# Two transformer layers on one core: an earlier first restack, idle products in batch 0, products and maxima placed elsewhere

## What is computed

```
# layer A: attention, 16 heads; queries are the normalised x itself (head size 8)
Q = heads(xn);  K = heads(xn @ Wk + bk);  V = heads(xn @ Wv + bv)      # value size 32
o = softmax(Q K^T + causal) V
x = x + (xn + gelu(o) @ Wf + bf)
# layer F: attention, 8 heads of 64, with 8 experts for the values and for the outputs
q, k = xn @ w_q, xn @ w_k;  gates = sigmoid(xn @ w_gate);  sel = argmax(gates)
gm = one_hot(sel) * gates
values = gm-weighted value_experts of xn
out = softmax(q k^T / 8 + causal) values
x = x + sum over heads and experts of gm * (out @ output_experts)
```

## Time and profile before

| | us |
|---|---|
| median of three plain runs (1241.27 to 1246.39) | 1242.96 |
| the profiled execution | 1249.98 |
| its span, first to last instruction | 1248.2 |
| TensorE, matmuls, busy | 1125.7 (90%) |
| TensorE, weight loads, busy | 636.2 (51%) |
| ScalarE busy | 945.1 (76%) |
| VectorE busy | 864.1 (69%) |
| GpSimd busy | 363.9 (29%) |
| mean share of full TensorE clock granted | 0.957 |

### The profile page before, as it was taken

The page is one execution under the profiler, slowest core; times in us unless marked ns, Lnnn a source line. Parts: engine busy times, 40 slices in busy tenths (PEclk is TensorE's granted clock), DMA queues, the critical chain, the costliest instruction groups (busy, mean ns, idle before and its releaser), DMA issues.

```text
span 1248.2 us, 19900 instructions
## 1 busy us (share of the span) xinstructions
PE 1125.7 (90%) x5720; PEld 636.2 (51%) x5720; DVE 864.1 (69%) x2715; ACT 945.1 (76%) x2639; POOL 363.9 (29%) x460
## 2 busy tenths in 40 slices
PE   2697998999989999999989999899999999899998
PEld 1124754357543764347543575437643475435753
DVE  4732878658676687758786686767877597866844
ACT  3874788956989489867889669894898678896651
POOL 1012323242133322342232421343223332323210
PEclk8556999989999999999999999999999999999999
DMA  6201223002320222202230023202222032300220
GB/s 192 67 10 71 69 84 90 11 15 69 111 59 12 58 65 78 59 4 69 86 95 10 20 65 111 59 12 60 64 77 59 4 75 85 91 3 24 56 69 9
DMA packets 43646, 72.73 MB, mean 58 GB/s; under 512 B 9664, under 2 KB 25408, under 8 KB 43216
## 3 DMA queue, kind: packets, MB, share of 16 engines
q1 hardware_dynamic: 42256, 67.26, 20.1%
q10 hardware_dynamic: 1280, 4.20, 1.2%
HBM read 45.34 MB, written 8.80 MB: 43 GB/s over the span
## 4 chain that ended last, share of the span: by engine, by line
PE 42%; ACT 30%; DVE 14%; issue 8%; DMA 3%; SPq 2%; POOL 2%; ACTq 0%; DVEq 0%
ACT masked L899 14%; PE ps_m L679 10%; ACT pt L950 10%; PE ps_o L667 8%; DVE masked L1275 6%; PE ps_max L576 3%; PE ps_exp L576 3%; PE ps_max L788 2%; PE ps_exp L578 2%; PE ps_m L485 2%; ACT s2k L839 2%; DVE val L1468 2%; POOL pt L1142 2%; ACT s2q L839 1%; DVE pt L1449 1%
## 5 line engine op out<-in xcount | busy, mean ns | idle before, releaser
L899 ACT ACTIVATE masked<-masked,low 128x512 f32<-128x512 f32 (+3 forms) x768 | 422.8, 553 | 73.3 <-DVE low L1275 71.6
L1275 DVE CUSTOM_DVE_ANT_0 masked<-ps_max,mask 128x512 f32<-128x512 f32 (+3 forms) x768 | 350.1, 487 | 158.0 <-PE ps_max L576 90.7
L1142 POOL TENSOR_SCALAR_AFFINE_SELECT pt<-pt 128x512 f32<-128x512 f32 (+2 forms) x192 | 144.8, 754 | 560.9 <-ACT pt L950 560.9
L950 ACT ACTIVATE pt<-ps_exp 128x384 f32<-128x384 f32 (+1 forms) x480 | 238.3, 517 | 63.4 <-PE ps_exp L576 35.4
L667 PE MATMUL ps_o<-pt,val 128*32 128x128 f32 (+6 forms) x1536 | 188.0, 471 | 15.4 <-POOL pt L1142 15.4
L576 PE MATMUL ps_max<-s2k,s1q 72*128 72x512 bf16 (+3 forms) x512 | 129.7, 321 | 49.6 <-DVE low L1275 29.3
L679 PE MATMUL ps_m<-at,oe_sb 128*128 128x512 f32 x300 | 157.6, 612 | 1.9 <-DVE at L1326 1.9
L899 ACT ACTIVATION_READ_ACCUMULATOR masked<-masked,low 128x1 f32 x768 | 146.1, 190 | 0.0
L576 PEld LDWEIGHTS ps_max<-s2k,s1q 72*128 72x128 bf16 x512 | 47.0, 99 | 144.7 <-DVE low L1275 72.1
L1326 DVE TENSOR_TENSOR at<-osb,hots 128x512 f32<-128x512 f32 x150 | 104.3, 700 | 14.0 <-PE ps_m L679 14.0
L576 PE MATMUL ps_exp<-s1q,s2k 75*128 75x384 bf16 (+3 forms) x384 | 99.2, 323 | 11.4 <-ACT pt L950 8.6
(11 more groups left out here) (183 smaller groups left out, 1960.8 us busy)
## 6 DMA issues: line engine op xcount, KB each, us to landing
hots<-hot_d SPq DMA_DIRECT2D x48, 256.0 KB, 4.5
s1q<-parts_q SPq DMA_DIRECT2D x96, 96.0 KB
s2k<-parts_k SPq DMA_DIRECT2D x96, 96.0 KB
s1q<-pt SPq DMA_DIRECT2D x64, 128.0 KB, 2.3
s1k<-pt SPq DMA_DIRECT2D x64, 128.0 KB, 2.3
hots<-hot_d ACTq DMA_DIRECT2D x16, 256.0 KB, 4.5
parts_q<-pt SPq DMA_DIRECT2D x24, 128.0 KB, 2.3
parts_k<-pt SPq DMA_DIRECT2D x24, 128.0 KB, 3.8
```

What stands on the lines that cost most here:

```text
L899: last = nc.scalar.activation(e, e, ACT.Exp, bias=low[:, g % 2, c:c + 1], scale=-1.0, accum_out=den[:, g % 2, c:c + 1])
L950: nc.scalar.activation(pt[:, (n % 2) * 4 + j, 0:c1 - c0], score_bank(k, u)[:, c0:c1], ACT.Exp).then_inc(exp_done[k].sem, 1)
L1142: nc.gpsimd.affine_select(out=v, in_=v, compare_op=ALU.is_ge, fill=0.0, base=0, pattern=[[0, HG[k]], [0, m], [1, P]], channel_multiplier=- ...
L1275: last = v.tensor_tensor_reduce(out=masked[:, u % JUNK, c0:c0 + w], in0=src[:, c0:c0 + w], in1=mask[:, S - w:S], scale=-1.0, scalar=POS, o ...
```

## The change

It has six parts. (1) Start: SyncE issues the zeros after the restacking and layer A of batch 0 no longer waits for them; the keys of group 0 of batch 0 are restacked by ScalarE's queue (`first_keys`). (2) Batch 0: Tensor gets `idle_product`, a matmul of constants into ps_m1 whose result nobody reads: six of 512 columns before layer A, one of 256 columns after each of the 36 units at the start, and wherever a later batch has a product of the batch before. (3) The products of layer A sit at other steps, evenly one a stage from step 7 on; the one between the two pieces of the projection goes before it. (4) `FIRST` holds 22 units, two at every step; the units 22 and 23 go on Tensor between the first value tile and the last weighing of layer F, and on Vector and Scalar to the start of layer A (`pre_units`). (5) The value tiles of layer A are spaced out among the units (`VALUE_AT`). (6) The first transposition of layer F uses bank 6.

```diff
 BANK.update({(k, "T", g): 0 for k in "AF" for g in range(GROUPS)})
+BANK["F", "T", 0] = 6
 BANK.update({("A", "V", t): (6, 2, 0, 3)[t] for t in range(T)})
...
 A_UNITS = STAGES * HG["A"]
-FIRST = {FIRST_AT + n: range(24 * n // 11, 24 * (n + 1) // 11) for n in range(11)}
+FIRST_UNITS = 22
+FIRST = {FIRST_AT + n: range(2 * n, 2 * n + 2) for n in range(11)}
...
-def pre_groups(a):
-    return (0, 1, 2) if a == 0 else (2,)
+FIRST_IDLE, IDLE = 6, 256
+VALUE_AT = {2: 0, 3: 1, 5: 2, 7: 3}
+def pre_units(a):
+    first = 0 if a == 0 else FIRST_UNITS
+    return [divmod(u, A_UNITS) for u in range(first, 3 * A_UNITS)]
...
 STEPS_AT = [("F", 14 + 5 * m // 4) for m in range(OUTPUTS_F)] + [("pre", n) for n in (2, 5, 8, 11)]
-STEPS_AT += [("A", u) for u in (1, 2, 4, 6, 8, 10, 13, 15, 18, 21)]
+STEPS_AT += [("A", u) for u in (1, 2, 4, 7, 11, 15, 19, 23, 27, 31)]
 for u, step in enumerate(STEPS_AT):
...
-PRODUCT_AT = 24
-LAST_AT = {36 + n: T * E - TURN + n for n in range(TURN)}
+PRODUCTS_AT = {35: T * E - TURN - 1, 39: T * E - TURN}
+LAST_AT = {(36 + n if n else 33): T * E - TURN + n for n in range(TURN)}
 NEXT_AT, NEXT_X_AT = 44, 28
-SUMS_AT = 6
+SUMS_AT = 8
 HOTS_AT = {4: (0,)}
...
             sp.dma_start(wf_sb[:], wf.rearrange("p (g d) -> p g d", d=D)).then_inc(w_in[1].sem, 16)
-            sp.wait_ge(cst.sem, cst.count(0, 16 * 3))
-            sp.dma_start(s2q[0:64].bitcast(F32).rearrange("p h n -> p (h n)"), zeros_d[0].partition_broadcast(64)
-                         ).then_inc(zero_rows.sem, 16)
...
             parts_to_dram(0, "q")
-            sp.wait_ge(zero_rows.sem, zero_rows.count(0, 16))
             parts_to_dram(0, "k")
+            sp.wait_ge(cst.sem, cst.count(0, 16 * 3))
             sp.wait_ge(parts_out["q"].sem, parts_out["q"].count(0, 16 * PARTS))
...
                 restack_q(g)
-                restack_k(g)
+                if g > 0:
+                    restack_k(g)
+            sp.dma_start(s2q[0:64].bitcast(F32).rearrange("p h n -> p (h n)"), zeros_d[0].partition_broadcast(64)
+                         ).then_inc(zero_rows.sem, 16)
             for b in range(B):
                 layer_a(b)
+                if b == 0:
+                    sp.wait_ge(zero_rows.sem, zero_rows.count(0, 16))
                 one_rows(b)
...
+            def idle_product(columns):
+                mm(ps_m[BANK["F", "acc", 0]][:, 0:columns], ident_sb[:],
+                   wf_sb[:].rearrange("p g d -> p (g d)")[:, 0:columns], start=True, stop=True)
...
+                if f < 0:
+                    idle_product(S)
+                    return
                 if u == 0:
...
                 n_units = STAGES * HG["A"]
-                for g in pre_groups(a):
-                    pe.wait_ge(restacked_a[g].sem, restacked_a[g].count(a, 16 * RESTACK["A"]))
-                    for n in range(n_units):
-                        if a > 0 and 1 <= n < T:
-                            value_a(a, n)
-                        if g == 2 and n == SCORES_AT:
-                            rows_arrived(a, 0)
-                            score_unit("A", a, 0, 0, 0)
-                            score_unit("A", a, 0, 0, 1)
-                        max_unit("A", a, g, n)
-                        if a > 0:
-                            outputs(a - 1, "pre", n)
-                        if a == 0 and g == 1 and n == n_units // 2 - 1:
-                            maxima_transposed("A", a, 0)
+                for n, (g, m) in enumerate(pre_units(a)):
+                    if a > 0 and n < 2:
+                        continue
+                    if m == 0:
+                        pe.wait_ge(restacked_a[g].sem, restacked_a[g].count(a, 16 * RESTACK["A"]))
+                    if a > 0 and VALUE_AT.get(n):
+                        value_a(a, VALUE_AT[n])
+                    if g == 2 and m == SCORES_AT:
+                        rows_arrived(a, 0)
+                        score_unit("A", a, 0, 0, 0)
+                        score_unit("A", a, 0, 0, 1)
+                    max_unit("A", a, g, m)
+                    if a > 0 and g == 2:
+                        outputs(a - 1, "pre", m)
+                    elif a == 0:
+                        idle_product(IDLE)
+                    if a == 0 and g == 1 and m == n_units // 2 - 1:
+                        maxima_transposed("A", a, 0)
                 for g in range(GROUPS):
...
                                 max_unit("A", a, 3, LATE[u])
-                            if a > 0 and OUTPUTS.get(("A", u)):
+                            if OUTPUTS.get(("A", u)):
                                 outputs(a - 1, "A", u)
-                            elif a > 0 and u == PRODUCT_AT:
-                                product(a - 1, T * E - TURN - 1)
+                            elif u in PRODUCTS_AT:
+                                product(a - 1, PRODUCTS_AT[u])
                             if s == 1 and j == 0 and g + 1 < GROUPS:
...
                             weigh("A", a, n - 1)
-                if a > 0:
-                    product(a - 1, T * E - TURN)
+                product(a - 1, T * E - TURN + 1)
                 weigh("A", a, NST - 1)
...
                     value_a(f + 1, 0)
+                    for g, m in pre_units(f + 1)[:2]:
+                        if m == 0:
+                            pe.wait_ge(restacked_a[g].sem, restacked_a[g].count(f + 1, 16 * RESTACK["A"]))
+                        max_unit("A", f + 1, g, m)
                 weigh("F", f, NST - 1)
...
                 f, first = a - 1, T * E - TURN
-                if f >= 0:
-                    product(f, first + 1)
-                project_back(a, (0, 1, 2))
-                if f >= 0:
-                    product(f, first + 2)
-                project_back(a, (3,))
-                if f >= 0:
-                    for u in range(first + 3, T * E - 2):
-                        product(f, u)
+                product(f, first + 2)
+                project_back(a, (0, 1, 2, 3))
+                for u in range(first + 3, T * E - 2):
+                    product(f, u)
                 transposed("F", a)
-                if f >= 0:
-                    product(f, T * E - 2)
-                    product(f, T * E - 1)
+                product(f, T * E - 2)
+                product(f, T * E - 1)
...
                 value_a(0, t)
-            pe.wait_ge(zero_rows.sem, zero_rows.count(0, 16))
             pe.wait_ge(set_v.sem, set_v.count(0, 3))
             pe.wait_ge(set_p.sem, set_p.count(0, 2))
+            pe.wait_ge(w_in[1].sem, w_in[1].count(0, 16 * 3))
+            for n in range(FIRST_IDLE):
+                idle_product(S)
             for b in range(B):
                 attention_a(b)
-                if b == 0:
-                    pe.wait_ge(w_in[1].sem, w_in[1].count(0, 16 * 3))
                 turn(b)
...
                 n_units = STAGES * HG[k]
-                for g in pre_groups(b) if k == "A" else ():
-                    for n in range(n_units):
-                        if g == 2 and n == SCORES_AT:
-                            weights(k, b, 0, 0)
-                            weights(k, b, 0, 1)
-                        denominators(k, b, g, n)
-                        if g == 1 and n == n_units // 2 - 1:
-                            maxima(k, b, 0)
-                    logs(k, b, g)
+                for g, m in pre_units(b) if k == "A" else ():
+                    if g == 2 and m == SCORES_AT:
+                        weights(k, b, 0, 0)
+                        weights(k, b, 0, 1)
+                    denominators(k, b, g, m)
+                    if b == 0 and g == 1 and m == n_units // 2 - 1:
+                        maxima(k, b, 0)
+                    if m == n_units - 1:
+                        logs(k, b, g)
                 if k == "F":
...
+            def first_keys():
+                act.wait_ge(cst.sem, cst.count(0, 16 * 3))
+                act.wait_ge(parts_out["k"].sem, parts_out["k"].count(0, 16 * PARTS))
+                n_rows, h = PARTS * DH, slice(0, HG["A"])
+                for m in range(PARTS):
+                    nc.scalar.dma_start(ks[m * n_rows:(m + 1) * n_rows, h],
+                                        parts_d["k"].rearrange("m d h n -> (m d) h n")[:, h]
+                                        ).then_inc(restacked_a[0].sem, 16)
+                nc.scalar.dma_start(ks[STACK:STACK + PARTS, h], onesb_d.rearrange("p (h n) -> p h n", n=S)[:, h]
+                                    ).then_inc(restacked_a[0].sem, 16)
...
             expert_weights_high()
+            first_keys()
             act.wait_ge(split_lo.sem, split_lo.count(0, 2))
...
                 turn(b)
+                if b == 0:
+                    act.wait_ge(zero_rows.sem, zero_rows.count(0, 16))
                 experts(b)
...
             def attention_a(a):
-                n_units = STAGES * HG["A"]
-                for g in pre_groups(a):
-                    for n in range(n_units):
-                        if a > 0 and n < T:
```

(18 more changed lines are left out.)

## The result

The changed kernel took 1226.22 us as a median of four plain runs (1224.75 to 1228.14), the kernel before 1243.82 beside it; the ratio is 0.9845 [0.9816, 0.9875]. The profiled execution took 1228.14, with a span of 1226.4 against 1248.2. The sign was right, the gain half of what was forecast: 17.6 instead of 36 in the medians, 21.8 instead of 35.8 between the profiled executions.

A forecast was written before the change was run, and what follows sets the result against it. Bounds: the start, batch 0 at 1.2 GHz, short waits of the fullest engine in steady batches. Terms 16.3+3.1+8.8+7.7+4.0 = 39.9, 35.8 after discount: 1214.2 profiled, 1207 plain; range 1191 to 1227.

The forecast's parts named there:

- Start: Opening of batch 0: without the wait for zeros and with a second issuer, Tensor starts earlier; 8.0 taken, 4.4 to 10.7.
- Rival C: Start of batch 0: it doesn't move, as competing restacked rows land in 13 instead of 5.15; 1215, chance 0.07.
- Clock of batch 0: Idle matmuls lift Tensor to 2.4 GHz: 8.9 gained in layer A, 2.4 behind it, 3.0 lost ahead of it.
- Rival B: Batch 0: idle work doesn't lift the clock and is paid at 1.2 GHz on a full engine; 1274, chance 0.04.
- Dip of batch 1: Low-clock dip ahead of batch 1's projection goes with more products in the last steps: 3.1, bounds 0 and 3.1.
- Bank: First transposition of layer F: Tensor's 1.47 wait for Scalar goes, Vector limits the gain; 0.5 a batch, 4.0 in all.
- Two units out: Three-unit steps 18 and 23 of layer F lose their waits: about 1.1 a batch, 7.7 over seven boundaries.
- Products spread: Layer A: fewer products ahead of step 24 shorten Scalar's waits, later ones fit Tensor's waits; 1.1 a batch, 8.8.
- The discount: Last three terms (20.5), gains of neighbouring waits, counted at four fifths, 16.4, as the next fullest engine takes over.
- Rival A: Steady batches stay bound by the fullest engine, only batch 0 gains: 1224, or 1231 with delayed last weights; chance 0.22.
- the two waits of 1.47 and 1.13: Signs in layer F: no 1.47 behind its first transposition, no 1.13 in the eighteenth step.
- the distance of the projections: Sign between two batches' projections: down from 145.4 to about 143; staying at 145 would mark the forecast wrong.

The follow-up runs named there:

- experiment 1: Changed kernel with the products back at their old places, all of part 3 undone, in batch 0 too: 1210.35 us, ratio 0.9709.
- experiment 5: Kernel before the change with only the products moved to the change's new places: 1259.87 us, ratio 1.0122.
- experiment 6: Changed kernel with the first transposition of layer F back in bank 0: 1232.68 us, ratio 0.9891.
- experiment 7: Changed kernel with all 24 units in layer F's steps again, none ahead of the last weighing, value tiles spaced from group 2: 1236.57 us, ratio 0.9918.
- experiment 10: Changed kernel with products at steps 5, 9, ... 37, without the six idle products before layer A and the 36 behind the units: 1204.99 us, ratio 0.9698.

## Why the prediction was half right

*Start: -8.0 forecast, -7.0 measured.* The steps held: key parts issued without waiting for the zeros, landing 3.11 (3.8 taken), restacking from 18.57 (19.7). Only the last landing was not the 5.15 taken over from before, but 7.37. Rival C's mechanism, a longer landing, is there in a small size: 2.2, not 8. In the other nine traces with this start the first maximum is at 25.9 to 27.8, so the forecast of 26.7 lies within what the start does from one execution to the next.

*Clock of batch 0.* The -8.9 for layer A proper is right where the products don't disturb it: with the old places (experiment 1) it is 36.3 in batch 0, 9.3 less than before. Turn and front of layer F gave 3.2 (2.4 forecast), the stretch ahead of the weights cost 2.0 (3.0). In sum 10.5 against the 8.3 forecast. Rival B is out: once the idle work had begun, the clock was at the lower level only from about 26 to 33.

*Dip of batch 1: 3.1 forecast.* That batch had been 1.8 longer in layer A and 1.3 in the turn than batch 2 before, and isn't now: 3.1. The size is right; the reason given, more products in the last steps, isn't shown. The kernel of experiment 5 has these products too, and its trace has dips in batches 4 and 6, of which this is the first:

```profile
657.80:664.70 6.90, 6.66 (x13) 2.94 (x14) 4.54 (x22) 5.73 (x20) 0.00 (x0) 0.51 0.13 30
```

*Bank: 4.0 forecast, 6.5 by the medians of experiment 6, 5.4 by its trace.* The mechanism held (next in line is Vector), the size was taken too low.

*Two units out: 7.7 forecast, 10.4 by the medians of experiment 7, 9.1 by its trace.* Also as described: 1.8 gained in layer F, where the waits of the earlier trace rows had counted for 1.7, and 0.5 lost behind it.

With the medians these five terms come to 37.5, against 31.1 forecast for them before the discount; less the 15.9 that follows they make 21.6, and 21.8 was measured between the profiled executions. That they meet so closely is chance: with the traces' 5.4, 9.1 and 16.2 they make 18.9, so the account closes to within 3 us and no better.

*Products spread: -8.8 forecast, +15.9 by experiment 1.* This is the step that failed, and alone it accounts for the miss. The prediction took 1.2 out of Scalar's waits in the first half because two products fewer stood ahead of step 24, and walked the late products through Tensor's waits ahead of weighings. Both steps looked at how much Tensor has to do, not at what stands next to what. The first product of the even row is at step 7, the last step of its stage, and each one after it four steps on, so each product joins a weighing. The waits that it had taken out (0.63, 0.43) grew to 1.49 and 0.99, though no more products stand ahead of the first than before and one fewer ahead of the second. The bounds of +1.4 to -0.9 a batch did not hold it either: the loss is 2.9 in layer A, with 0.6 of it regained in the turn. That regained 0.6 is the product gone from the projection, for which 0.86 had been set. (The five waits of 1.4 in all that the prediction counted in the first half are three in the trace, 1.23 in all; the sign would have been wrong with either.)

*The discount.* A fifth was taken off because neighbouring waits compensate each other. Bank and units, the two terms with a wait of one engine for another that was freed, came in above their full size. The measured 1226 lies just inside the upper end of the range, 1227, and that is luck: the range got there by every gain coming in small, whereas three of the gains (clock, bank, units) came in above their size and one term, forecast as a gain, was a loss.

*Rival A (only batch 0 gains, 1224 or 1231)* names nearly the right time with the wrong content. Layer F of the steady batches did gain, 18.1 in all; layer A proper lost. Its addition, late products that delay the last weights, is near to what happens, but the loss begins at the seventh step, not at the thirty-first: 1.2 of the 2.9 fall in the first half of the layer (Scalar busy 16.89 instead of 18.11).

Of the signs that the prediction named, the first maximum near 27, the clock and the two waits of 1.47 and 1.13 came out as it said. Scalar's waits at the start of layer A grew where they were to go, and from first to last weights layer A of batch 0 took 38.3 where it said 35. And the distance of the projections stayed at 145 (144.8), which it had named as the mark of a wrong forecast.

## What to carry to other kernels

Filler work on a busy engine is to be judged by what it stands next to. Before moving it, write down for each place how long the engine then goes without feeding its consumer (here product 0.86 plus weighing 1.0), and set that against what the consumer has in its buffers. The number of fillers in a stretch says little: the same count in the same even row was worth +15.9 or -5.1 us against the old places, by two steps of offset.

## What was not expected of the hardware

Raising the clock was worth little where another engine sets the pace: experiment 10 runs from about 21 to 59 at 0.50 and is as fast as the kernel that pays 42 idle products to avoid it. And with the six idle products done by 22.4 and 5.3 of waiting behind them, layer A still began at the lower level. The stretch of it in the changed kernel, then the one after:

```profile
26.70:33.50 6.80, 5.80 (x17) 3.94 (x18) 2.75 (x11) 3.20 (x10) 0.00 (x0) 0.53 0.43 127
33.60:45.00 11.40, 10.70 (x56) 7.17 (x55) 10.60 (x50) 10.96 (x42) 0.00 (x0) 1.00 0.64 128
```
